# Last expert stage: each expert's weights in four transfers of 2 KB rows, and full and small places in turn

## The chip, the cores and the metric

One core of a Trainium2 chip runs the whole program. The metric is the device time of one execution in microseconds (us); lower is better. TensorE (PE) multiplies matrices, VectorE (DVE) and ScalarE (ACT) work on tiles, GpSimd (POOL) also issues the indexed transfers, and SyncE (SP) issues the plain ones. All transfers run on the core's 16 DMA engines.

## The reference

Two decoder layers over 32 sequences of 128 tokens with 256 features each, all in f32. Only the last part matters here: a mixture of experts in which each token goes to two of eight experts.

```python
xf = x.reshape(T, D)
gate_scores = jax.nn.sigmoid(gate_logits + balance_bias)
topk_scores, topk_idx = jax.lax.top_k(gate_scores, ACTIVE_EXPERTS)
...
h = jax.nn.silu(jnp.einsum('td,ehd->teh', xf, w1))
expert_out = jnp.einsum('teh,edh->ted', h, w2)
out = jnp.einsum('te,ted->td', comb, expert_out)
...
x = x + _L1_ffn_ref(_layernorm(x, axis=-1), ...)
```

Each expert has w1 of 512 x 256 and w2 of 256 x 512, together 1024 KB.

## The kernel before

The kernel runs its stages one after the other: a Mamba block, two attention blocks, a first expert stage (names with d_), a recurrence, an attention block (e_), and the last expert stage (f_). The last stage reuses the memory of earlier tiles, so nearly everything in it is called e_dead in the profile; its function is `list_experts`.

The rows of tokens were scattered before into `rows_in_place`, one region for each expert. The stage works through 40 **places** (`SLOTS`, numbered u = 0 to 39). A full place takes two tiles of 128 rows of one expert, a small place takes one. `list_plan` writes the list `PLACE_PLAN` of pairs (tiles, number of the first half unit): 21 full places from a first table that is filled early (`EARLY`), then, from the second table, 10 full places (u = 21 to 30) and 9 small ones (u = 31 to 39). Which expert and which rows a place has is only known at run time; some places are empty, and then all of their row numbers are out of bounds and nothing is added to the output. Empty places load their weights and compute all the same.

For each place u:

- SP loads its rows (272 KB for a full place, 136 KB for a small one, L2677) and its expert's weights (1024 KB in one transfer, 8 KB in each of 128 partitions, L2680) into a ring of `RING` = 3 buffers. The weights wait until PE has finished the down product of place u - 3, since they overwrite its buffer.
- PE makes the four up products (L2718, f = 0 to 3). After f = 0 of place u it makes the down product of place u - 1 (L2705, `output_tensor`), and after f = 1 it transposes the rows of place u + 1 (L2695, `turn_rows`). Each up product starts with a wait for the weights at f = 0.
- ACT applies SiLU (L2741) and copies the transposed rows (L2731).
- DVE reads each token's number (`f_token`, L2756) and multiplies each tile of the down product by the token's share (L2764, one for each tile). It writes into a ring of `OUT` = 4 buffers and waits there for the additions of place u - 4.
- POOL adds the tile to the output in memory by an indexed transfer with addition (L2778, two for a full place, one for a small one). It waits first until all additions of the places before have landed, since two places can hold the same token. The end of the program waits for the last of them.

```python
            for u in range(SLOTS):
                pl.wait_ge(mixed, upto[u + 1])
                ...
                after(pl, added, 16 * upto[u])
                for k in range(tiles[u]):
                    nc.gpsimd.indirect_dma_start(tokens_of, ...
```

Of the kernel before, what the change touches and what calls it, by code (L numbers as in the profile page):

```python
# [27 lines left out]
def after(eng, sem, count):  # L28

    if not isinstance(count, int) or count > 0:  # L30
        eng.wait_ge(sem, count)
# [97 lines left out]
def early_units(groups):  # L129

    rows = 2 * (groups - 1) * GT
    return -(-(rows - 8 * (UR - 1)) // UR)


def list_plan(groups):

    early = early_units(groups)
    halves = (2 * groups * GT - 8) // 128 + 8 - 2 * early
    single = 8 + halves % 2
    full = (halves - single) // 2  # L140
    plan = [(2, 2 * n) for n in range(early)] + [(2, 2 * n) for n in range(full)]
    return early, full, plan + [(1, 2 * full + n) for n in range(single)]


def slot_order(groups):
# [31 lines left out]
def decoder_kernel(nc, ins, out):  # L177
# [18 lines left out]
    E, REGION = 8, NG * GT  # L196
    RUNS = 2 * E + 1
    EARLY, FULL, PLACE_PLAN = list_plan(NG)
    SLOTS = len(PLACE_PLAN)
    PLACES = sum(split_units(NG)) - split_units(NG)[1] // 2  # L200
# [19 lines left out]
    w_in = m_w_sb[:, 0:1024].rearrange("p (k o) -> p k o", k=KD)  # L220
# [488 lines left out]
    def early_router(tag, mem, table, FB, SB, number, full, empty, x_in, plan):  # L709
# [236 lines left out]
        def late_table_vector(dve, at):  # L946
# [45 lines left out]
                  early=[16, 30, 48]),  # L992
# [8 lines left out]
    def attention(tag, turn, sets, relu=False, rms=None, out_w=None, table=None, result=None, ahead=None, begun=None, then=None, shared=None, base=0):  # L1001
# [721 lines left out]
        if table:  # L1723
            out_late = LAST["out_at"]
            last_sides = [lambda pe, p: [back_tensor(pe, NG - 1, p, [0], LAST["back"]), router["total_tensor"](pe, 0, LAST["total"])],
                          lambda dve, p: [back_vector(dve, NG - 1, p, [0], out_late), router["early_table_vector"](dve, LAST["early_table"])],
                          lambda act, p: [], lambda pool, p: []]
            end_sides = [lambda pe: [back_tensor(pe, NG - 1, 1, [1], LAST["back"]), router["total_tensor"](pe, 1, LAST["late_total"])],
                         lambda dve: [back_vector(dve, NG - 1, 1, [1], out_late), router["late_table_vector"](dve, LAST["late_table"])],
                         lambda act: [], lambda pool: []]  # L1730
            turn_of_list = turn + 4
            places = list_experts("f", mem, 0, table, result, dead, router, lambda sp: store_x(sp, NG - 1),
                                  ended=dict(mixed=(mixed, PAIRS * NG), drawn=(drawn, PAIRS * NG), shifted=(shifted, UNITS * NG),
                                             taken=(taken, UNITS * NG), valued=(valued, PAIRS * (NG - 1))))
            listed_places = [places[x] for x in ("tensor", "vector", "scalar", "pool")]
# [890 lines left out]
    def list_experts(tag, mem, turn, table, result, dead, router, store_rest, ended):  # L2626

        FC, UT = 4, UR // 128
        UPS, WN = KD * 512, KD * 512 + 4 * D
        RING, OUT = 3, 4  # L2630
        left = list(sem_set[turn])
        s = lambda name: ctx.enter_context(nc.semaphore(f"{tag}_{name}", num=left.pop(0)))
        t = lambda name, shape, dtype=F32: mem.take(f"{tag}_{name}", shape, dtype)
        w = dead[0][:, 0:RING * WN].rearrange("p (r n) -> p r n", r=RING)
# [10 lines left out]
        w_in, row_in = ([s(f"{n}{r}") for r in range(RING)] for n in ("w_in", "row_in"))  # L2645
# [17 lines left out]
        def sync(sp):  # L2663
            for u in range(SLOTS):
                r = u % RING
                if u == 0:
                    sp.wait_ge(ended["valued"][0], ended["valued"][1])
                    sp.wait_ge(in_list[0], ALL)
                    sp.wait_ge(in_list[1], ALL - 16 * router["scatters"])
                    sp.wait_ge(ready_places, 1)  # L2670
                if u == EARLY:
                    sp.wait_ge(in_list[1], ALL)
                    sp.wait_ge(ready_places, 2)
                after(sp, turned, u - RING + 1)
                after(sp, sent_to, u - RING + 1)
                at = sp.value_load(table["start_i"][:].unsqueeze(2)[0:1, u], min_val=0, max_val=E * REGION // 128)
                sp.dma_start(rows[:, r, 0:tiles[u]], rows_at[:, bass.ds(at, tiles[u])]).then_inc(row_in[r], 16)  # L2677
                e = sp.value_load(table["expert_i"][:].unsqueeze(2)[0:1, u], min_val=0, max_val=E - 1)
                after(sp, down, late(u - RING + 1))
                sp.dma_start(w[:, r], ins[f"{tag}_w"][e]).then_inc(w_in[r], 16)  # L2680
                if u == RING:
                    store_rest(sp)
            sp.wait_ge(stored, 16 * NG)

        def turn_rows(pe, u):
            pe.wait_ge(row_in[u % RING], 16 * (u // RING + 1))
            if u == 0:
                pe.wait_ge(ended["shifted"][0], ended["shifted"][1])
            if u == 1:
                pe.wait_ge(ended["mixed"][0], ended["mixed"][1])  # L2690
                pe.wait_ge(ended["drawn"][0], ended["drawn"][1])
            after(pe, turned_in, u)
            for c in range(KD):
                for k in range(tiles[u]):
                    step = nc.tensor.transpose(TB(u)[:, c, k * L:k * L + L], rows[:, u % RING, k, c * 128:c * 128 + 128], ident[:])  # L2695
            step.then_inc(turned, 1)

        def output_tensor(pe, u):
            pe.wait_ge(hidden, FC * u + FC)
            if u == 0:  # L2700
                pe.wait_ge(ended["taken"][0], ended["taken"][1])
            for r in range(tiles[u]):
                after(pe, mixed, had(u, r))
                for f in range(FC):
                    step = nc.tensor.matmul(DB(r), hid[:, u % 2, f, r * 128:r * 128 + 128], w_down[:, u % RING, f], start=f == 0, stop=f == FC - 1)  # L2705
                step.then_inc(down, 1)

        def tensor(pe):
            turn_rows(pe, 0)
            yield 0  # L2710
            for u in range(SLOTS):
                for f in range(FC):
                    if f == 0:
                        pe.wait_ge(w_in[u % RING], 16 * (u // RING + 1))
                        pe.wait_ge(turned_in, u + 1)
                    after(pe, hidden, FC * (u - 1) + f + 1)
                    for c in range(KD):
                        step = nc.tensor.matmul(UB(f)[:, 0:wide(u)], w_up[:, u % RING, c, f * 128:f * 128 + 128], xT[:, u % 2, c, 0:wide(u)], start=c == 0, stop=c == KD - 1)  # L2718
                    step.then_inc(up, 1)
                    if f == 0 and u:  # L2720
                        output_tensor(pe, u - 1)
                    if f == 1 and u + 1 < SLOTS:
                        turn_rows(pe, u + 1)
                    yield 10 * u + 2 * f + 2
            output_tensor(pe, SLOTS - 1)
# [41 lines left out]
        def pool(pl):  # L2767
# [13 lines left out]
            pl.wait_ge(added, 16 * upto[SLOTS])  # L2781

        return dict(sync=sync, tensor=tensor, scalar=scalar, vector=vector, pool=pool)


# [7 lines left out]
    u = lambda name, shape: u_mem.take(f"u_{name}", shape)  # L2793
# [16 lines left out]
    f = lambda name, shape, dtype=F32: f_mem.take(f"f_{name}", shape, dtype)  # L2810
# [191 lines left out]
```

## Time and profile before

| | |
|---|---|
| median of 3 runs | 3130.05 us (3126.87 to 3141.59) |
| the profiled execution, its time | 3133.9 us |
| its span | 3131.8 us |
| granted clock, mean | 0.952 of full |
| PE busy | 2695.4 us (86%) |
| last stage, first weights asked for to end | about 2834 to 3131.8 us |

The profile shows one execution. "Busy" is the time in which an engine executes; an engine's idle time before an instruction is put down to what released it. Times inside the trace count from the start of the span. DMA shares are of 16 engines: 50% means that each engine moved packets half of the time.

### The profile page before, as it was taken

To read this page: it belongs to the slowest core of one execution; us is meant where nothing else is said; L and a number is where in the kernel's file an instruction comes from. 1 tells how busy PE (TensorE), PEld (TensorE's weight loads), DVE (VectorE), ACT (ScalarE), POOL (GpSimd) and SP (SyncE) were. 2 spreads that over 40 slices of the span, in tenths; PEclk is the share of its full clock that TensorE was granted. 3 is DMA by queue.
4 is the path that set the end of the run, shared out by engine and by line. 5 is a ranking of instruction groups with operands and counts; after the bars stand their busy time and mean duration, and the time that the engine had idled before them with its cause. 6 is when DMAs were issued, how large, how long until landed. Compare 5 with 4: busy or idle time off the path is not lost.

```text
span 3131.8 us, 49455 instructions
## 1 busy us (share of the span) xinstructions
PE 2695.4 (86%) x16576; PEld 1837.2 (59%) x16576; DVE 1900.0 (61%) x3513; ACT 1523.1 (49%) x2641; POOL 1499.7 (48%) x1619
## 2 busy tenths in 40 slices
PE   5888888876988888879999999899888888878997
PEld 2333333323666566645788887697455555557886
DVE  3788888784888788863222222501688988883211
ACT  4566665553777666630122221443666666643322
POOL 3577666673555577625322222200345555553443
PEclk8999999988999999989999999899999999978998
DMA  9700000001005000002377775200000100006875
GB/s 324 245 0 1 0 1 1 1 0 37 15 20 190 1 1 0 1 22 95 117 212 209 209 212 146 71 1 1 1 18 30 37 33 31 22 20 188 228 216 167
DMA packets 137955, 244.73 MB, mean 78 GB/s; under 512 B 15936, under 2 KB 111424, under 8 KB 127040
## 3 DMA queue, kind: packets, MB, share of 16 engines
q1 hardware_dynamic: 111168, 207.61, 20.1%
q0 software_dynamic: 26592, 34.63, 5.6%
q8 instruction: 109, 1.79, 0.2%
q14 instruction: 86, 0.70, 0.1%
HBM read 151.28 MB, written 92.73 MB: 78 GB/s over the span
## 4 chain that ended last, share of the span: by engine, by line
PE 35%; DVE 6%; issue 6%; POOL 5%; ACT 2%; DMA 1%; another core or an unknown queue 0%; POOLq 0%; DVEq 0%; ACTq 0%
PE PS L2442 11%; PE PS L2398 6%; PE PS L2066 4%; PE PS L2705 3%; PE PS L2718 3%; POOL e_hs L1544 2%; DMA out<-e_dead,f_token 1%; DVE e_mx L1447 1%; POOL e_qs L1547 1%; PE PS L1399 1%; POOL rows_in_place L878 1%; PE PS L2057 1%; PE PS L1337 1%; DVE e_pr L1451 1%; DVE e_den L1458 1%
## 5 line engine op out<-in xcount | busy, mean ns | idle before, releaser
L578 POOL TENSOR_TENSOR u_in<-dtx,b_rep 128x512 f32<-128x512 f32 x256 | 325.4, 1294 | 201.3 <-ACT b_rep L559 200.1
L594 DVE TENSOR_TENSOR_SCAN state<-PS,u_in 128x512 f32<-128x512 f32 x256 | 312.3, 1220 | 59.3 <-POOL u_in L578 34.9
L551 PE MATMUL PS<-scaled,ident 128*128 128x512 f32 x512 | 295.6, 661 | 28.7 <-DVE scaled L588 28.7
L2459 ACT ACTIVATE d_act_b<-PS 128x256 f32<-128x256 f32 (+2 forms) x192 | 76.5, 400 | 446.4 <-PE PS L2442 426.4
L1544 POOL TENSOR_TENSOR e_hs<-e_pr 128x512 f32<-128x512 f32 x128 | 163.0, 1273 | 236.5 <-ACT e_pr L1511 232.9
L1544 POOL TENSOR_TENSOR u_hs<-u_pr 128x512 f32<-128x512 f32 x128 | 166.3, 1299 | 215.1 <-ACT u_pr L1511 214.6
L2442 PE MATMUL PS<-d_unit_T,d_w 128*128 128x256 f32 (+1 forms) x1280 | 260.6, 356 | 1.1 <-ACT d_unit_T L2452 1.1
L2362 POOL DMA_INDIRECT out_by_token<-d_y_rows,d_token x71 | 110.8, 1561 | 300.2 <-DVE d_y_rows L2489 201.6
L2468 DVE TENSOR_TENSOR d_hid<-d_act_b,PS 128x256 f32<-128x256 f32 (+2 forms) x192 | 84.4, 441 | 279.9 <-ACT d_act_b L2459 245.6
L567 ACT ACTIVATE PS<-dt,decay_rate 128x508 f32<-128x508 f32 x256 | 173.4, 686 | 138.0 <-DVE state L594 136.2
L2442 PEld LDWEIGHTS PS<-d_unit_T,d_w 128*128 128x128 f32 x1280 | 221.0, 190 | 26.3 <-DVE d_hid L2468 1.3
L588 DVE TENSOR_TENSOR scaled<-state,PS 128x512 f32<-128x512 f32 x256 | 169.4, 664 | 55.9 <-PE PS L532 44.3
L1447 DVE TENSOR_REDUCE u_mx<-PS 128x8 f32<-128x1024 f32 x128 | 155.9, 1218 | 67.9 <-PE PS L1390 67.8
L2398 PE MATMUL PS<-d_w,d_hid 128*128 128x256 f32 x824 | 186.8, 380 | 3.6 <-DVE d_hid L2468 2.6
L2778 POOL DMA_INDIRECT out<-e_dead,f_token x71 | 110.8, 1561 | 158.1 <-DVE f_token L2756 68.2
L1507 ACT ACTIVATE e_pT<-PS 128x1024 f32<-128x1024 f32 x128 | 130.8, 1022 | 103.2 <-PE PS L1399 103.2
L1447 DVE TENSOR_REDUCE e_mx<-PS 128x8 f32<-128x1024 f32 x128 | 155.8, 1217 | 40.6 <-PE PS L1390 40.5
L2398 PEld LDWEIGHTS PS<-d_w,d_hid 128*128 128x128 f32 x824 | 155.6, 190 | 30.2 <-issue 7.5
L1399 PE MATMUL PS<-ident,e_pr 128*128 128x128 f32 x1024 | 148.2, 292 | 25.8 <-ACT e_pr L1511 25.3
L1507 ACT ACTIVATE u_pT<-PS 128x1024 f32<-128x1024 f32 x128 | 131.2, 1025 | 74.2 <-PE PS L1399 73.9
L551 PEld LDWEIGHTS PS<-scaled,ident 128*128 128x128 f32 x512 | 97.2, 204 | 117.9 <-DVE scaled L588 87.1
L1451 DVE TENSOR_TENSOR u_pr<-PS,u_mx 128x1024 f32<-128x1024 f32 x128 | 156.7, 1224 | 9.3 <-POOL u_hs L1544 2.2
(453 smaller groups left out, 6145.2 us busy)
## 6 DMA issues: line engine op xcount, KB each, us to landing
d_w<-in_d_w SPq DMA_DIRECT2D x42, 1024.0 KB, 5.8
e_dead<-in_f_w SPq DMA_DIRECT2D x40, 1024.0 KB
rows_in_place<-blank SPq DMA_DIRECT2D x136, 272.0 KB, 4.1
d_w<-in_d_w SPq DMA_DIRECT2D x42, 512.0 KB
rows_by_expert<-zeros SPq DMA_DIRECT2D x36, 272.0 KB, 3.1
d_unit_rows<-rows_by_expert SPq DMA_DIRECT2D x31, 272.0 KB
e_dead<-rows_in_place SPq DMA_DIRECT2D x31, 272.0 KB
X<-in_x SPq DMA_DIRECT2D x8, 512.0 KB, 11.2
```

What stands on the lines that cost most here:

```text
L551: nc.tensor.matmul(YB[:, c], ident[:], scaled[:, (KD * n + c) % RC], start=False, stop=n == NS - 1).then_inc(m_y, 1)
L567: nc.scalar.activation(seqs(DECAY[:, k % RD])[:, :, 1:L], seqs(dt[:, p, c])[:, :, 1:L], ACT.Exp, scale=decay_rate[:, c * NS + n:c * NS + n ...
L578: nc.gpsimd.tensor_tensor(u_in[:, k % RU], dtx[:, p, c], b_rep[:, n % RB], ALU.mult).then_inc(m_u, 1)
L588: nc.vector.tensor_tensor(scaled[:, k % RC], state[:, k % 2], CB, ALU.mult).then_inc(m_hc, 1)
L594: nc.vector.tensor_tensor_scan(state[:, k % 2], DECAY[:, k % RD], u_in[:, k % RU], 0.0, ALU.mult, ALU.add).then_inc(m_h, 1)
L1399: step = nc.tensor.transpose(TR[:, m], pr[:, i % 2, m], ident[:])
L1447: nc.vector.tensor_reduce(mx[:, i % 2], scores_of(i), AX.X, ALU.max).then_inc(maxed, 1)
L1451: nc.vector.tensor_tensor(pr[:, i % 2], scores_of(i), mx[:, i % 2].unsqueeze(2).broadcast_to([128, MAPS, L]), ALU.subtract).then_inc(shift ...
L1507: nc.scalar.activation(pT[:, i % 2].rearrange("p h q -> p (h q)"), flat(PS[:, 4:6]), ACT.Copy).then_inc(taken, 1)
L1544: nc.gpsimd.tensor_tensor(hs[:, i % 2], pr[:, i % 2, :, 0:L // 2], pr[:, i % 2, :, L // 2:L], ALU.add).then_inc(halved, 1)
L2398: step = nc.tensor.matmul(out_h[:, n], hid[:, p, f, row:row + 128], w_down[:, r, f], start=f == 0, stop=f == FC - 1)
L2442: step = nc.tensor.matmul(b, wt[:, r, c, f * 128:f * 128 + 128], x, start=c == 0, stop=c == KD - 1)
```

## The change

Two edits. The weights of a place come in four transfers of 512 columns (256 KB, 2 KB in each partition) in place of one, and PE waits for all four. And in the second table the small places stand between the full ones: after u = 22 they take turns, small, full, small, and so on to u = 39, which is small. The number of places, the half units that they name and the sums stay as they are.

```diff
     single = 8 + halves % 2
     full = (halves - single) // 2
-    plan = [(2, 2 * n) for n in range(early)] + [(2, 2 * n) for n in range(full)]
-    return early, full, plan + [(1, 2 * full + n) for n in range(single)]
+    plan = [(2, 2 * n) for n in range(early)]
+    pairs, ones = [(2, 2 * n) for n in range(full)], [(1, 2 * full + n) for n in range(single)]
+    alone = max(full - single, 0)
+    plan += pairs[:alone]
+    for n in range(single):
+        plan += pairs[alone + n:alone + n + 1] + ones[n:n + 1]
+    return early, full, plan
...
-        RING, OUT = 3, 4
+        RING, OUT, PARTS = 3, 4, 4
...
-                sp.dma_start(w[:, r], ins[f"{tag}_w"][e]).then_inc(w_in[r], 16)
+                for c in range(PARTS):
+                    part = slice(c * WN // PARTS, (c + 1) * WN // PARTS)
+                    sp.dma_start(w[:, r, part], ins[f"{tag}_w"][e][:, part]).then_inc(w_in[r], 16)
...
-                        pe.wait_ge(w_in[u % RING], 16 * (u // RING + 1))
+                        pe.wait_ge(w_in[u % RING], 16 * PARTS * (u // RING + 1))
```

PE before, at the passage from the last full place (u = 30) to small ones near the end of the program (L2718 up product, L2705 down product, L2695 transposes of the next rows; 128x256 is a full place's up product and 128x128 a small one's):

```order
L2718 MATMUL PS<-e_dead 128x256 x2
L2695 MATMUL PS<-ident,e_dead 128x128 x2
L2718 MATMUL PS<-e_dead 128x256 x4
L2718 MATMUL PS<-e_dead 128x128 x2
L2705 MATMUL PS<-e_dead 128x256 x8
L2718 MATMUL PS<-e_dead 128x128 x2
L2695 MATMUL PS<-ident,e_dead 128x128 x2
L2718 MATMUL PS<-e_dead 128x128 x6
L2705 MATMUL PS<-e_dead 128x256 x4
```

PE after, near the end of the program (line numbers are 7 higher):

```order
L2725 MATMUL PS<-e_dead 128x256 x2
L2702 MATMUL PS<-ident,e_dead 128x128 x2
L2725 MATMUL PS<-e_dead 128x256 x4
L2725 MATMUL PS<-e_dead 128x128 x2
L2712 MATMUL PS<-e_dead 128x256 x8
L2725 MATMUL PS<-e_dead 128x128 x2
L2702 MATMUL PS<-ident,e_dead 128x128 x4
L2725 MATMUL PS<-e_dead 128x128 x4
L2725 MATMUL PS<-e_dead 128x256 x2
L2712 MATMUL PS<-e_dead 128x256 x4
```

What before stood there once now stands nine times: a small place's first up product ahead of a full place's down product, and in the small place the transposes of a full place's rows (x4).

SP before, one small place (f_start_i and f_expert_i are the tables of starts and experts; the waits name semaphores by their numbers' first owners):

```order
L2676 TENSOR_LOAD f_start_i [waits m_nb,m_padded]
L2676 ISA x2
L2677 ISA
L2677 DMA e_dead<-rows_in_place 128x272
L2678 TENSOR_LOAD f_expert_i
L2678 ISA x2
L2680 ISA [waits m_vec2]
L2680 DMA e_dead<-in_f_w 128x2048
```

SP after, the same place's weights:

```order
L2687 ISA [waits m_vec2]
L2687 DMA e_dead<-in_f_w 128x512
L2687 ISA
L2687 DMA e_dead<-in_f_w 128x512
L2687 ISA
L2687 DMA e_dead<-in_f_w 128x512
L2687 ISA
L2687 DMA e_dead<-in_f_w 128x512
```

One wait still stands ahead of the weights; three transfers more stand behind it, ahead of the rows of the next place.

## Rows read from the trace of the kernel before

**Rows 1.** Busy time by stretch (columns PE, PEld, DVE, ACT, POOL, clock, DMA share, GB/s).

```profile
3000.00:3050.00 50.00, 50.00 (x247) 44.05 (x246) 9.04 (x35) 15.37 (x42) 20.66 (x14) 1.00 0.76 218
```

**Rows 2.** PE in order of time (start, duration): a full place's parts, down products, waits.

```profile
3001.89 0.60 PE L2695 MATMUL PS<-ident,e_dead 128*128 128x128 f32 x4
3002.33 2.76 PE L2718 MATMUL PS<-e_dead 128*128 128x256 f32 x12
3004.92 3.62 PE L2705 MATMUL PS<-e_dead 128*128 128x256 f32 x16
...
3063.69 3.62 PE L2705 MATMUL PS<-e_dead 128*128 128x256 f32 x16
...
3070.59 3.72 PE L2705 MATMUL PS<-e_dead 128*128 128x256 f32 x16
...
3076.23 1.99 PE L2705 MATMUL PS<-e_dead 128*128 128x256 f32 x8
...
3084.06 1.99 PE L2705 MATMUL PS<-e_dead 128*128 128x256 f32 x8
...
3105.46 0.71 PE L2718 MATMUL PS<-e_dead 128*128 128x128 f32 x4 [0.90 <-DMA e_dead<-in_f_w]
3109.60 1.99 PE L2705 MATMUL PS<-e_dead 128*128 128x256 f32 x8 [0.37 <-ACT e_dead L2741]
```

**Rows 3.** DVE: the second tile of u = 30.

```profile
3074.35 0.48 DVE L2764 TENSOR_SCALAR e_dead<-PS,f_share_rows 128x256 f32<-128x256 f32 x1 [1.14 <-PE PS L2705]
```

**Rows 4.** POOL's indexed additions in order of time, with the idle time before.

```profile
3017.74 1.55 POOL L2778 DMA_INDIRECT out<-e_dead,f_token  x1 [4.49 <-DMA out<-e_dead,f_token]
...
3041.08 1.56 POOL L2778 DMA_INDIRECT out<-e_dead,f_token  x1 [0.30 <-issue]
3047.72 1.55 POOL L2778 DMA_INDIRECT out<-e_dead,f_token  x1 [5.08 <-DMA out<-e_dead,f_token]
...
3075.67 1.55 POOL L2778 DMA_INDIRECT out<-e_dead,f_token  x1 [3.10 <-DVE f_token L2756]
...
3123.12 1.55 POOL L2778 DMA_INDIRECT out<-e_dead,f_token  x1 [2.02 <-DMA out<-e_dead,f_token]
```

**Rows 5.** The chain that ended last: additions (start, time from issue to landing).

```profile
3077.53 5.92 DMA out<-e_dead,f_token
3084.31 3.82 DMA out<-e_dead,f_token
3088.99 7.26 DMA out<-e_dead,f_token
...
3107.06 3.82 DMA out<-e_dead,f_token
...
3119.54 2.72 DMA out<-e_dead,f_token
```

**Rows 6.** DMA queues (packets, MB, share) in 3075.67:3084.2, then in 3119.54:3123.1.

```profile
q1 hardware_dynamic: 598, 2.56, 80.8%
q0 software_dynamic: 288, 0.00, 1.9%
...
q0 software_dynamic: 144, 0.00, 2.0%
```

**Rows 7.** Other loads: queue q1 in 792:798 (one 512 KB load), then SP.

```profile
q1 hardware_dynamic: 272, 0.52, 25.1%
...
993.89 12.37 SPq L2863 DMA_DIRECT2D out_by_token<-zeros  x16
...
747.08 0.43 SPq L1134 DMA_DIRECT2D c_wk<-in_c_wk  x1
747.55 0.53 SPq L1134 DMA_DIRECT2D c_wv<-in_c_wv  x1
```

**Rows 8.** The first weights: SP's issue, and PE's weight load that waited for them.

```profile
2833.86 0.37 SPq L2680 DMA_DIRECT2D e_dead<-in_f_w  x1
2839.90 1.93 PEld L2718 LDWEIGHTS PS<-e_dead 128*128 128x128 f32 x8 [0.62 <-DMA e_dead<-in_f_w]
```

## The prediction

> **What bounds the kernel now.** I read the page first, then the busy time by stretch, PE in order of time, POOL in order of time and the chain that ended last. The change touches only the last stage, from about 2834 us to the end at 3131.8. In its middle PE is busy in all of the 50 us between 3000 and 3050, at full clock, while the DMA engines stand at a share of 0.76 [rows 1]. The down products of u = 21 and u = 29 start at 3004.92 and 3063.69 [rows 2]: eight full places in 58.77 us, 7.35 us each, with no gap. From the starts at 3001.89, 3002.33 and 3004.92 [rows 2], transposes take 0.44, three up products 2.59 (0.86 each), and the down product the other 3.45; a small place's parts are half of it, some 0.45, 0.22 and 1.73, together 3.74. No transfer decides there.
>
> The end is different. PE starts its last down product at 3109.60 [rows 2] and is done at 3111.6, but the last addition is only issued at 3123.12 [rows 4]. The chain runs over additions, one after another [rows 5]. Call L the time from the issue of a place's last addition to its landing. POOL starts the next place 0.86 us after a landing: 3084.31 + 3.82 = 3088.13, next start 3088.99 [rows 5]. So a small place takes POOL 0.86 + L, and a full one 1.86 us more for its first addition (3077.53 less 3075.67, [rows 4, 5]). With L = 3.8 to 7.3, nine small places in a row need 4.7 to 8.1 us each; PE makes one in 3.915 us (3076.23 to 3084.06 for two, [rows 2]). POOL falls behind through the whole run, and the program ends with POOL: 3123.12 + 2.72 for an empty place as in [rows 5] = 3125.8, and 6 us of closing after it.
>
> **What lengthens L.** Two empty places compare directly. The addition at 3077.53 belongs to u = 30, which moved 0.00 MB [rows 6], and took 5.92 us. The one at 3119.54 is empty too, with nothing beside it, and took 2.72 [rows 5, 6]. The difference is 3.20 us. Each addition is 144 packets, 9 on each of 16 engines [rows 6]. Beside the first, queue q1 used 80.8% of 8.53 us for 2.56 MB, 0.16 MB an engine: 6.9 us, or 0.35 us for 8 KB. Nine packets that each wait behind one 8 KB weight packet wait 3.15 us. That is the difference. With 2 KB rows the same count gives 9 x 0.09 = 0.8 us.
>
> **The change, part by part.** (1) *2 KB rows.* Engine time per byte: the 512 KB load of 2 KB rows took 25.1% of 6 us on q1, 1.5 us, so 350 GB/s [rows 7]; the 8 KB rows above ran at 0.16 MB in 6.9 us on 16 engines, 370 GB/s, partly other packets. I take no loss; the bound above is 6% of some 3 us a place, which PE's full places hide. Separate transfers do not queue badly either: 16 stores of 256 KB were issued in 12.37 us [rows 7], 0.77 us each.
>
> (2) *SP.* Issues without a register read stand 0.47 us apart [rows 7]. Three more for each place cost 1.4 us, and the register step ahead of each some 0.03. The last quarter of the weights is asked for 1.4 us later; SP then takes the next rows. In turns, the weights of a full place have 11.3 us less the 1.95 of a small down product and 0.86 of an up product, 8.4 us; those of a small place 11.3 - 3.6 - 0.45 = 7.2 us. The longest wait shown is that of u = 39, whose weights were needed at 3104.5 and came at 3105.46 [rows 2]. The first weights of the stage took 6.04 us with the ring otherwise nearly empty (2833.86 to 2839.90) and PE's weight load waited 0.62 us for them [rows 8]. At worst 6.04 + 1.4 = 7.4 exceeds 7.2 by 0.2, nine times: 0 to 2 us; I take 0, since the queue moves the first quarters while SP issues the last. At the stage's start the cover is thin: 0 to 1.4 us, I take 0.5. If it slipped at each of 40 places it would be 56 us, but a full place has 10 us for it (7.35 x 2 less 3.6 and 0.86) and hides it.
>
> (3) *The turns, on PE.* In the small run PE lost 2.3 us to weights: from 3084.06 to 3109.60 are 25.54 us, against 6 x 3.915 less the 0.22 of the last place's missing transposes, 23.27 [rows 2]. These waits go. Against it, a small up product (0.45 us) is now the only cover ahead of a full down product: from 3063.69 to 3070.59 are 6.90 us [rows 2] where shorter work (7.35 - 0.43 - 0.22) gives 6.70, 0.2 lost on ACT. That happens nine times, not once, but the small places' own ACT gap of 0.17 goes with each (3.915 against 3.74): +0.03 for each pair, so 11.29 us a pair. PE's last tile is handed to POOL at about 3110.3: that of u = 22 starts at 3004.92 + 7.35 - 0.22 = 3012.05 (before: 3012.27), that of u = 38 at 3012.05 + 8 x 11.29 = 3102.4, then 3.45, three small up products with ACT's gap 1.86, and 2.61 to DVE's end.
>
> (4) *The turns, on POOL.* A full place hands over its tiles 4.24 us after its down product starts (3070.59 to 3074.35 + 0.48 = 3074.83, [rows 2, 3]), and POOL starts 0.84 later [rows 4]. A pair needs (0.86 + 1.86 + L) + (0.86 + L) = 3.58 + 2L of POOL against 11.29 of PE. They are equal at L = 3.86. Which L? The lone addition at 3107.06 took 3.82 with data [rows 5]; that is the floor. In the full places before, L reached 5.8 (3041.08 to 3047.72 less 0.86, [rows 4]); it was about 4.6 on the average of the twelve from 2985 on, as near as their waits show, 0.8 over the floor where 3.2 were possible. A quarter of that, for 0.8 possible, is 0.2, so **L = 4.05**, and 3.0 for places with little or nothing in them.
>
> From u = 22, whose additions start at 3017.74 [rows 4], to the end POOL has nine full places (9 x 1.86 = 16.7), 17 steps of 0.86 (14.6), 14 places with data and 4 short ones (u = 35 and the last three): 3017.7 + 31.3 + 14 x 4.05 + 4 x 3.0 = **3117.7**. Sum: 3125.8 becomes 3117.7 + 0.5 from the start = 3118.2, that is -7.6 us; with a small lag in both, -7. The profiled execution of 3133.9 would be 3127; it lies 3.9 us above the median, so against 3130.05 the forecast is **3123 us**, -0.22%.
>
> **A rule against it.** The 256 KB transfers of [rows 7] stand 0.77 us apart. The Trainium skill ("DMA: Bandwidth & Descriptors", section Bandwidth) says to batch transfers to at least 1 MiB to reach three quarters of the peak; its section on the anatomy of one DMA fits 2.0 us plus the bytes at 436 GB/s to each, for GpSimd's transfers. An estimate from that page for four quarters in series is 4 x 2.6 = 10.4 us against 4.4 for one transfer. By that rule the change would lose if the fixed parts added up; the trace's 0.77 us shows them overlapped.
>
> **Rivals.**
> - *L stays near 4.6* (3.7 when empty), because additions wait for something other than packet length. For it: 7.26 at 3088.99 [rows 5] is more than floor plus 3.15. Against: the two empty places. End: 3017.7 + 31.3 + 64.4 + 14.8 = 3128.2, later than before by 2.4: 3133. Nothing gained, the turns having moved POOL's lag forward.
> - *Weights late in the turns.* Price 0.5 to 1 us for each pair through PE and 1.4 at the start: PE's end 3115 to 3119, the end 3121 to 3126; time 3126 to 3132.
> - *Slower: transfers in series.* If a quarter's fixed time adds up (say the 2.7 us of an empty addition [rows 5] for each of three more, 8.1 us), weights take 14 us against the 10 us of a full place and PE waits 4 us at some 38 places: +150 us, 3280. It decides from 4 us more a transfer. [Rows 7] speak against.
> - *POOL never lags* (L = 3.82, 2.72): the end is PE's, 3102.4 + 4.24 + 0.84 + 1.86 + 2.72 + 0.86 + 2.72 = 3115.6. That is -10: 3120.
> - *Only the turns act, and well.* Without the short rows, L with data at 4.6 and empty at 3.5: 3127.4, that is +1.6; so this can't give a gain.
>
> **How the numbers follow.** Chances: forecast 0.50 (3120 to 3126, its own range), no lag 0.10 (3118 to 3121), L unchanged 0.18 (3129 to 3135), weights late 0.14 (3126 to 3132), transfers in series 0.04, something that the rows don't show 0.04. The medians themselves spread (3126.87 to 3141.59 in three runs), which widens both ends. The range 3118 to 3133 leaves out the series case, half of the unknown, and the top of the unchanged one. 0.5% is 15.7 us, about what a measurement here can tell from no change. More than 12 us can't come from this part: PE's last work stands at 3110. So faster by over 0.5% has 0.03, slower 0.06, within it 0.91.
>
> **What would show it.** In the new profile: the additions' landing times around 4 us instead of up to 7.3; POOL's last start within 6 us of PE's last matmul, not 11.5; no wait of L2725 for in_f_w in the second table; pairs of 11.3 us on PE; q1's packets in the stage four times as many, with the same engine time. The first weights' wait grows from 0.62 to about 1. Wrong would be: L of 4.6 and more beside 2 KB packets, a DMA share of the full places above 0.9, or waits for weights in them.

## The result

Before: median 3131.12 us (3125.62 to 3141.59, 15 runs). After: **3146.11 us** (3138.51 to 3149.08, 15 runs), ratio **1.0039** with the 95% interval 1.003 to 1.0047. By the ratio the kernel is some 12 us slower (the medians lie 15 us apart) where 7 us less were forecast, and the time lies above the range. The change does what it says: the turns and the four transfers are there. The kernels of the experiments ran on several chips, whose medians of the kernel before lie between 3131 and 3140 us; so they are compared by their ratios to it.

The profiled execution took 3149.08 us. Its page and its busy time by stretch (PE, PEld, DVE, ACT, POOL, clock, DMA share, GB/s):

```profile
span 3147.3 us, 49815 instructions
PE 2703.6 (86%) x16576; PEld 1842.9 (59%) x16576; DVE 1901.9 (60%) x3513; ACT 1522.3 (48%) x2641; POOL 1499.6 (48%) x1619
```

```profile
3000.00:3050.00 50.00, 49.73 (x263) 43.59 (x262) 9.76 (x38) 14.57 (x48) 17.90 (x13) 1.00 0.87 235
3050.00:3100.00 50.00, 42.88 (x233) 37.24 (x231) 8.13 (x33) 13.86 (x47) 14.73 (x10) 1.00 0.73 197
3100.00:3106.00 6.00, 5.85 (x22) 4.96 (x23) 0.00 (x0) 0.28 (x1) 1.69 (x2) 0.72 0.96 235
```

PE has the same 16576 matmuls. From 3000 to 3050 it is as busy as in [rows 1]; in the next 50 us it idles for 7. PE in order of time, which answers to [rows 2]:

```profile
3005.68 3.62 PE L2712 MATMUL PS<-e_dead 128*128 128x256 f32 x16
3012.58 3.72 PE L2712 MATMUL PS<-e_dead 128*128 128x256 f32 x16
...
3024.09 3.72 PE L2712 MATMUL PS<-e_dead 128*128 128x256 f32 x16
...
3083.16 0.71 PE L2725 MATMUL PS<-e_dead 128*128 128x128 f32 x4 [1.52 <-DMA e_dead<-in_f_w]
...
3091.92 1.13 PE L2725 MATMUL PS<-e_dead 128*128 128x256 f32 x4 [2.82 <-DMA e_dead<-in_f_w]
...
3100.15 0.79 PE L2725 MATMUL PS<-e_dead 128*128 128x128 f32 x4 [2.56 <-DMA e_dead<-in_f_w]
3100.73 5.27 PE L2712 MATMUL PS<-e_dead 128*128 128x256 f32 x16
...
3116.49 0.71 PE L2725 MATMUL PS<-e_dead 128*128 128x128 f32 x4 [3.00 <-DMA e_dead<-in_f_w]
...
3124.05 1.99 PE L2712 MATMUL PS<-e_dead 128*128 128x256 f32 x8 [0.37 <-ACT e_dead L2748]
```

The first pair (3012.58 to 3024.09) takes 11.51 us, close to the forecast 11.29. Then weights come late, four times by 1.5 to 3.0 us. After the first two of these waits the granted clock stays at 1.00 (3083 to 3095). After the last two it falls (0.72 from 3100 to 3106, 0.50 of it from 3101 to 3103, which is the 1.2 GHz level), and a full down product takes 5.27 us in place of 3.62. PE starts its last down product at 3124.05, 14.45 us later than in [rows 2]. POOL is later still: its last addition goes out at 3138.60, against 3123.12 in [rows 4], and is again what the end waits for. The additions in the chain that ended last (start, time to landing), from u = 22 on, which answer to [rows 5]:

```profile
3020.40 6.91 DMA out<-e_dead,f_token
...
3028.17 6.30 DMA out<-e_dead,f_token
...
3037.18 4.18 DMA out<-e_dead,f_token
...
3051.17 6.77 DMA out<-e_dead,f_token
...
3083.73 7.99 DMA out<-e_dead,f_token
...
3092.58 5.14 DMA out<-e_dead,f_token
...
3100.43 7.35 DMA out<-e_dead,f_token
...
3135.02 2.73 DMA out<-e_dead,f_token
```

The chain has one such row for each of the 17 places u = 22 to 38. The first eleven sum to 68.5 us, so **L = 6.2 us** on the average where the forecast had 4.05; the other six are 3.6 to 3.8 with data and 2.7 without. All 17 sum to 87.7 us; with 2.7 for u = 39, 90.4, against the forecast 68.7. That is 21.7 us of the 23.6 by which the last landing (3138.60 + 2.7 = 3141.3) misses the forecast 3117.7. The rest is the start (0.8) and 1 us between landings and next additions.

Two sides of the same lag, from the waits in the stage, 2835 to 3147 (engine, line, what was waited for: us in total, times, longest):

```profile
POOL out L2785 <- DMA out<-e_dead,f_token: 93.8, 25, 6.2
DVE f_token L2763 <- DMA out<-e_dead,f_token: 45.7, 9, 9.7
...
PE PS L2725 <- DMA e_dead<-in_f_w: 10.4, 6, 3.0
```

How DVE's wait reaches PE is seen around 3083 to 3092. First DVE, then SP, in order of time:

```profile
3081.04 0.15 DVE L2763 CAST f_token<-e_dead 128x1 int32<-128x1 f32 x1 [4.86 <-DMA out<-e_dead,f_token]
...
3091.75 0.17 DVE L2763 CAST f_token<-e_dead 128x2 int32<-128x2 f32 x1 [9.67 <-DMA out<-e_dead,f_token]
```

```profile
3020.98 1.88 SPq L2687 DMA_DIRECT2D e_dead<-in_f_w  x4
...
3032.49 1.88 SPq L2687 DMA_DIRECT2D e_dead<-in_f_w  x4
...
3051.16 1.88 SPq L2687 DMA_DIRECT2D e_dead<-in_f_w  x4
...
3083.14 1.88 SPq L2687 DMA_DIRECT2D e_dead<-in_f_w  x4
3092.72 0.33 SPq L2682 DMA_DIRECT2D e_dead<-rows_in_place  x1
3093.81 1.88 SPq L2687 DMA_DIRECT2D e_dead<-in_f_w  x4
```

The addition of 3083.73 lands at 3091.72. At 3091.75 DVE may read the next token numbers, since the ring of `OUT` = 4 was full; that releases the row buffer, SP asks for the next rows at 3092.72 and, behind them in its order, for weights at 3093.81. PE needs those and gets them at 3100.15. So once POOL is four places behind, the landings of the additions set when weights are asked for.

### The profile page after: what moved, and what is told of

It is laid out like the page before. It is cut to its first block, busy times and chain, and to the rows that moved or that the text cites. A ratio compares the mean times of both kernels' runs of the same rounds, so it can differ in the third digit from the quotient of the medians.

```text
span 3147.3 us, 49815 instructions
## 1 busy us (share of the span) xinstructions
PE 2703.6 (86%) x16576; PEld 1842.9 (59%) x16576; DVE 1901.9 (60%) x3513; ACT 1522.3 (48%) x2641; POOL 1499.6 (48%) x1619
## 4 chain that ended last, share of the span: by engine, by line
PE 29%; POOL 7%; issue 7%; DVE 7%; DMA 6%; ACT 2%; POOLq 0%; SPq 0%; DVEq 0%; ACTq 0%
PE PS L2447 11%; PE PS L2403 6%; DMA out<-e_dead,f_token 5%; PE PS L2071 4%; POOL e_hs L1549 3%; POOL e_qs L1552 1%; DVE e_mx L1452 1%; POOL out L2785 1%; PE PS L1404 1%; POOL rows_in_place L883 1%; PE PS L2062 1%; DVE e_pr L1456 1%; PE PS L1342 1%; DVE e_den L1463 1%; PE PS L2712 1%
## 5 line engine op out<-in xcount | busy, mean ns | idle before, releaser
L1404 PEld LDWEIGHTS PS<-ident,e_pr 128*128 128x128 f32 x1024 | 125.5, 151 | 63.0 <-ACT e_pr L1516 55.1
```

Source lines behind the costliest of these rows:

```text
L1404: step = nc.tensor.transpose(TR[:, m], pr[:, i % 2, m], ident[:])
```

## The experiments

**1. Each edit alone.** `e1_turns` has the new order and one transfer (`PARTS = 1`); `e2_parts` has the order of before and four transfers.

```diff
-        RING, OUT, PARTS = 3, 4, 4
+        RING, OUT, PARTS = 3, 4, 1
```

> Only the turns; the weights come in one transfer of 8 KB rows as before. Theory A (an addition waits for the whole weight burst that is already queued, whatever its rows; the turns put a full place's second addition right behind the next weights, so POOL needs more than PE's 11.3 us a pair, falls four places behind, and then DVE's read of the token numbers and with it SP's next rows and weights wait): 8 to 16 us slower than before, with the same PE waits for weights of 1 to 3 us in the last pairs. Theory B (the quarters make the weights late, the turns are harmless): within 3 us of before.

> Only the four transfers of 2 KB rows; the order of places as before. Theory A: 0 to 4 us slower than before (the start 0.7, and later weights in the run of small places). Theory B: 10 to 16 us slower. Were the prediction's step on packets right (short packets let additions through), it would be 3 to 6 us faster.

Measured: e1_turns 1.0063 (1.005 to 1.0076); e2_parts 1.0006 (0.9995 to 1.0017). The loss belongs to the turns: some 20 us, more than the 8 to 16 that theory A gave. The four transfers of 2 KB rows take a part of it back when they are there; alone they are worth nothing that can be told. In the chain of e1_turns the last additions of u = 22 and u = 26 (start, time to landing):

```profile
3022.59 9.50 DMA out<-e_dead,f_token
...
3056.56 8.63 DMA out<-e_dead,f_token
```

Over u = 22 to 32 the eleven rows of that chain give L = 6.8 (74.7 / 11). In the chain of e2_parts the eight full places u = 22 to 29 have L = 4.5 (36.1 / 8). The forecast's step from 4.6 to 4.05 was worked out for just such places, and it is not there. And the empty place u = 30, on whose two additions the forecast was built, in the chain of e2_parts and in its DMA queues from 3074.41 to 3081.7:

```profile
3069.49 4.07 DMA out<-e_dead,f_token
...
3076.27 5.36 DMA out<-e_dead,f_token
...
3082.48 5.87 DMA out<-e_dead,f_token
```

```profile
q1 hardware_dynamic: 1201, 2.07, 93.2%
q0 software_dynamic: 288, 0.00, 2.2%
```

Beside 2 KB rows it took 5.36 us; the forecast's count of packets gives 2.72 + 0.8 = 3.5, and 8 KB rows had 5.92 [rows 5]. So an addition does not wait for one weight row with each of its packets.

**2. The changed kernel again, and with a deeper ring.** `after_again` is the changed kernel, on the chip of experiment 4. `e3_out8` is the changed kernel with eight output buffers, `e7_turns_out8` the same with one transfer, `e10_before_out8` the kernel before with eight.

```diff
-        RING, OUT, PARTS = 3, 4, 4
+        RING, OUT, PARTS = 3, 8, 4
...
-        y = dead[1][:, 3072:5120].rearrange("p (o k d) -> p o k d", o=OUT, k=UT)
+        y = dead[1][:, 3072:7168].rearrange("p (o k d) -> p o k d", o=OUT, k=UT)
```

> The changed kernel itself, beside the others on one chip. All theories: 8 to 16 us slower than before (it measured a ratio of 1.0039), the turns alone having been 1.0063.

> The changed kernel with eight output buffers in place of four (OUT = 8), so DVE and SP are held only when POOL is eight places behind. Theory A: PE's waits for weights in the last pairs (some 10 us in all) go, and the end is POOL's chain alone: 4 to 10 us faster than the changed kernel, still not faster than before. Theory B: no change against the changed kernel, the waits for weights stay.

> The turns alone (8 KB rows) with eight output buffers in place of four. Theory A: the coupling through the output buffers turns POOL's lag into PE waits, so without it PE's waits for weights fall from some 9 us to below 3, and the loss against before falls from 20 us to 8 to 14 us, what is left being POOL's chain of long landings. Rival (weights late for a reason of their own): PE's waits stay at 9 us and the time at that of e1_turns.

> The order and the transfers of before, with eight output buffers in place of four. In before, PE waits some 2 us for weights in the run of small places, behind DVE's held read of token numbers. Theory A: these waits go, but the end is POOL's chain, so the time is within 3 us of before. Rival (before, too, loses through the coupling): 4 us or more faster.

Measured: after_again 1.0052 (1.0035 to 1.0069); e3_out8 1.004 (1.0026 to 1.0053); e7_turns_out8 1.0027 (1.0009 to 1.0045); e10_before_out8 0.9993 (0.9976 to 1.001). With eight buffers DVE's read of the token numbers waits no more, and in the turns PE loses nothing more to late weights. In e7_turns_out8 the first weights were asked for 4.7 us earlier than in [rows 8] (2829.20), and PE starts its last down product 4.8 us earlier than in [rows 2]: PE needs just as long. Yet POOL, shown behind it, is 25 us later than PE:

```profile
3104.82 1.99 PE L2712 MATMUL PS<-e_dead 128*128 128x256 f32 x8 [0.37 <-ACT e_dead L2748]
```

```profile
3129.77 1.55 POOL L2785 DMA_INDIRECT out<-e_dead,f_token  x1 [2.02 <-DMA out<-e_dead,f_token]
```

So in the turns the waits of PE are a consequence: they go, and POOL's chain of additions still makes the turns slower than before. The order of before is different. There e10_before_out8 has the time that was expected, but PE's waits for weights didn't go: 4.9 us in three waits, against 1.9 in the profile before. With DVE's waits gone they are still there, so theory A had their cause wrong. The longest, 2.8 us, ends at 3078.51, and from 3074 to 3078 the DMA engines are busy throughout (a share of 1.01). The ring of four buffers does add to the loss in the one-transfer kernel (1.0063 against 1.0027, intervals apart). In the changed kernel itself the medians don't show it (1.0039 and 1.0052 against 1.004, where 4 to 10 us were expected), though L over u = 22 to 32 falls from 6.2 to 5.5 in the profile (60.1 / 11); its share there stays open.

**3. Row length and number of transfers apart.** `e4_rows2k` has the order of before and one transfer of 2 KB rows, the weights being laid out in memory as four blocks; `e9_turns_1of2k` the same in the turns; `e8_turns_4of8k` has the turns and four transfers of 32 partitions with 8 KB rows.

```diff
-                sp.dma_start(w[:, r], ins[f"{tag}_w"][e]).then_inc(w_in[r], 16)
+                sp.dma_start(w[:, r].rearrange("p (c n) -> p c n", c=4), ins[f"{tag}_w"][e].rearrange("c p n -> p c n")).then_inc(w_in[r], 16)
```

```diff
-                    part = slice(c * WN // PARTS, (c + 1) * WN // PARTS)
-                    sp.dma_start(w[:, r, part], ins[f"{tag}_w"][e][:, part]).then_inc(w_in[r], 16)
+                    part = slice(32 * c, 32 * c + 32)
+                    sp.dma_start(w[part, r], ins[f"{tag}_w"][e][part]).then_inc(w_in[r], 16)
```

> One transfer for a place's weights as before, but cut into 2 KB rows by the layout in memory (four blocks of 512 columns for each expert); the order of places as before. Theory A: the size of a row changes nothing, within 2 us of before, additions beside weights still take up to 6 to 7 us to land. The prediction's step: landings beside weights at 4.5 us at most, 3 to 6 us faster than before.

> The turns with four transfers for a place's weights, each of 32 partitions with 8 KB rows (the changed kernel has four of 128 partitions with 2 KB rows). So far the turns cost 0.63% with one transfer of 8 KB rows and 0.39 to 0.52% with four of 2 KB rows. If the number of transfers is what lets additions in between, this kernel is like the changed one (12 to 17 us slower than before); if the length of a row is, it is like the turns alone (18 to 24 us slower). I expect the number.

> The turns with one transfer for a place's weights, in 2 KB rows (blocks in memory as in e4_rows2k). If the number of transfers counts: 18 to 24 us slower than before, landings up to 9 us. If the length of a row counts, as the prediction had it: 12 us or less.

Measured: e4_rows2k 0.9994 (0.9981 to 1.0006); e8_turns_4of8k 1.0082 (1.0057 to 1.0106); e9_turns_1of2k 1.0047 (1.0032 to 1.0063). The number of transfers, which I had expected to count, does nothing here that can be told. In the turns it is the rows that count: 1.0063 and 1.0082 with 8 KB, 1.0039 to 1.0052 with 2 KB, each with one and with four transfers. On one chip e8 and e9 have medians of 3160.12 and 3146.94 us. The loss of e9, 15 us, lies between the two that were expected. L over u = 22 to 32, in one profile of each, says the same: 6.8 and 6.9 (75.4 / 11 in e8) with 8 KB, 6.2 and 6.4 (70.1 / 11 in e9) with 2 KB. A quarter of the row length takes off some 0.5 us, where the forecast's count wanted three quarters of all that lies above the floor. In the order of before it is worth nothing; there the empty place u = 30 took even 6.42 us beside 2 KB rows of one transfer.

**4. Without the weights.** Both load only 32 of the 2048 columns of the weights; the loads of rows, 136 or 272 KB a place, are left. `e6_before_light` has the order of before, `e5_turns_light` the turns, each with one transfer.

```diff
-                sp.dma_start(w[:, r], ins[f"{tag}_w"][e]).then_inc(w_in[r], 16)
+                sp.dma_start(w[:, r, 0:32], ins[f"{tag}_w"][e][:, 0:32]).then_inc(w_in[r], 16)
```

> The turns with one transfer for a place's weights that brings only 32 of the 2048 columns (the other weights are left out, so the output is not the reference's); PE's and POOL's work is the same. Theory A (the loss comes from additions that wait for weight bursts): landings of 2.7 to 3.8 us everywhere, a pair takes POOL 11.2 us against PE's 11.3, no waits for weights; 8 to 12 us faster than before and 2 to 6 us faster than e6_before_light. Rival (the turns cost by themselves, through ACT, DVE or the order of waits): at least 8 us slower than e6_before_light.

> The order of before with the same 32 columns of weights alone (the rest is left out). Theory A: the run of small places costs POOL 4.7 us each in place of 4.7 to 8.1; 4 to 8 us faster than before. Rival: if bursts do not lengthen landings, within 3 us of before.

Measured: e5_turns_light 0.9967 (0.9953 to 0.9981), e6_before_light 0.9966 (0.9949 to 0.9983). Without weights the turns lose nothing, so they hurt by where they put the additions beside the weights. They win nothing either: the gain of 2 to 6 us over e6_before_light that was expected even here is not there to be measured. On PE it has a reason. The pair of places takes 11.51 us in e5_turns_light too (down products at 3017.04 and 3028.55), 0.22 more than the forecast's 11.29. From the first up product to the start of the last down product PE needs 269.6 us there, in e6_before_light 267.5 and before 269.7: the turns cost PE about what its waits for weights had cost it, and in e5_turns_light the chain that ended last runs over PE. The lowest L shows in the chain of e6_before_light, from the same empty place u = 30 on, behind u = 28 and u = 29:

```profile
3064.52 5.15 DMA out<-e_dead,f_token
3072.39 3.83 DMA out<-e_dead,f_token
3078.93 2.80 DMA out<-e_dead,f_token
3082.59 3.69 DMA out<-e_dead,f_token
3087.13 3.61 DMA out<-e_dead,f_token
3091.59 3.86 DMA out<-e_dead,f_token
3096.31 3.73 DMA out<-e_dead,f_token
```

2.80 us, against 5.92, 5.36 and 6.42 with weights in one or the other form; and u = 31 to 34 at 3.6 to 3.9, where before had up to 7.26 [rows 5]. There the difference is due to the weights. But not all is: u = 28 and u = 29 have the same L with the weights as without. Before, in the chain that ended last:

```profile
3063.12 5.17 DMA out<-e_dead,f_token
3071.01 3.81 DMA out<-e_dead,f_token
```

In these two places of the row of full ones, the weights that were asked for 3.0 and 3.5 us ahead of the addition add nothing, and shorter rows have nothing to win. In u = 25 they do add: 5.8 before [rows 4], at most 4.6 here (3042.49 to the next start at 3047.97, less 0.86). What makes the 5.2 of u = 28 stays open. Leaving out the weights is worth 0.34% in all.

The empty place u = 30 also shows that the moment counts. In e10_before_out8, with full weights in 8 KB rows, its second addition comes late, 7.0 us after one place's weights were asked for (3074.30) and 1.5 us ahead of the next (3082.80):

```profile
3081.35 2.72 DMA out<-e_dead,f_token
```

That is as short as with nothing beside it. Before, 3.1 us after weights and 0.9 ahead of the next, it took 5.92.

**5. The weights spread out in time.** By now I held that an addition suffers from a burst: 1 MB asked for at once. Then four quarters spread over the place should let it through. `e11_turns_spread` (from the changed kernel) and `e12_before_spread` (from e2_parts) hold back each of the last three quarters until PE has made a certain up product of place u - 2 or, for the last quarter, of place u - 1.

```diff
                 for c in range(PARTS):
+                    if u >= RING and c:
+                        sp.wait_ge(up, FC * (u - 2) + (0, 2, 4, FC + 1)[c])
                     part = slice(c * WN // PARTS, (c + 1) * WN // PARTS)
```

> The changed kernel, with the four quarters of a place's weights spread in time: SP waits with the second for up product f = 1 of place u - 2, with the third for f = 3, with the last for f = 0 of place u - 1. Theory A (an addition waits behind the weights queued as one burst): a burst is at most two quarters, 1.5 us in place of 3, so landings stay below some 5 us, POOL falls behind by less than four places, and the loss against before falls from 12 to 17 us to between -4 and +6 us. Rival (only the share of the DMA engines counts, not how it is bunched): as the changed kernel.

> The order of before with the four quarters spread in the same way. Theory A: landings of full places below 4.5 us; in the run of small places the weights may come late, since a last quarter has 3.9 us less the down product. Between 4 us faster and 6 us slower than before. Rival: as e2_parts, within 3 us of before.

Measured: e11_turns_spread 1.0125 (1.0099 to 1.0151), e12_before_spread 1.0127 (1.0098 to 1.0156), both some 38 us slower than before, and alike. The theory of the burst fell, and so did both rivals, that nothing would change. SP and then the chain of additions in e12_before_spread, in the first table and, the last row, at u = 24:

```profile
2940.23 4.55 SPq L2684 DMA_DIRECT2D e_dead<-in_f_w  x4
...
2947.58 4.22 SPq L2684 DMA_DIRECT2D e_dead<-in_f_w  x4
```

```profile
2972.32 6.26 DMA out<-e_dead,f_token
...
2981.30 5.58 DMA out<-e_dead,f_token
...
2989.59 5.39 DMA out<-e_dead,f_token
...
3061.09 7.29 DMA out<-e_dead,f_token
```

A place's weights are now asked for over 4.2 to 4.6 of the 7.35 us of a full place, and every place's second addition meets them: L = 5.4 to 6.6 in the full places from 2972 to 3033, and up to 7.35 later. The places from 2972.32 to 2981.30 and on to 2989.59 take POOL 9.0 and 8.3 us against PE's 7.35, so POOL falls behind from the first table on. The order of the places no longer matters. POOL is late first and PE only then. In e12_before_spread PE runs from 2850 to 3038 without a wait for weights, while DVE's reads of token numbers wait for additions from 2978.61 on. Behind that PE waits 33.1 us for weights, in e11_turns_spread 26.5. Whether these waits would go with eight buffers was not tried; in the run of small places the late last quarter may cost time by itself. What the first table shows is that the same bytes, asked for over a longer time, made L longer, not shorter.

## Why the prediction was wrong

**The step that failed** is "What lengthens L", and with it the **L = 4.05** of step (4). The difference of two empty places (3.20 us) agreed with nine waits of 0.35 us, and I took the agreement for the mechanism. It was a coincidence: with 2 KB rows the same place took 5.36 and 6.42 us, not 3.5. Shown: L is 2.7 to 2.8 (empty) or mostly 3.6 to 3.9 (data, once 5.15) without weights; with them it is 3.7 to 9.7, 6.2 on the average of the changed kernel's first eleven places from u = 22 on; shorter rows take off some 0.5 us in the turns and nothing in the order of before.

**The phase.** The forecast carried one L from the row of full places into the turns. What goes with a long L is when the place's last addition goes out against the weights. In the row of full places of e2_parts the weights of 3065.96 were asked for 3.53 us before the addition of 3069.49, which took 4.07. In the turns: weights at 3020.98 and an addition at 3020.40, 6.91; at 3051.16 and 3051.17, 6.77; at 3083.14 and 3083.73, 7.99; but 3032.49 and 3037.18, 4.7 us behind them, 4.18. It is no strict rule: at 3058.79, 3.1 us behind the weights, L is 5.85. SP's quarters go out when a down product ends. After a full place's product its second addition follows some 3.5 us later; in the turns the small place's product that ends next asks for weights just then. PE's order fixes this phase, and where POOL lags and `OUT` = 4 binds, the landings themselves do. That both coincide is seen in the rows. That the weights beside the additions are the price was shown by taking them out (experiment 4), and the empty place at two moments fits it; how L follows from the distance was not measured by itself.

**The step that was missing** is the price of a lag. A pair asks 3.58 + 2L of POOL; with L = 6.2 that is 16 us against PE's 11.5. The five pairs from the addition at 3020.40 to the one at 3100.43 took 16.0 us each. The forecast knew that the two break even at L = 3.86, a hair from the floor, and so had no margin. What follows when POOL is four places behind (DVE, SP, weights, PE, clock) it left out.

**The rivals.** "L stays near 4.6" was nearest: no gain from short rows, POOL's lag moved forward. Its L was right for the order of before (4.5 in e2_parts) and wrong for the turns, and so was its price, 2.4 us instead of 15.5. "Weights late in the turns" came true (10.4 us of waits in place of 2.3), but by POOL's lag, not by slower transfers, and POOL's own end lies later still. "Transfers in series" did not come: e2_parts is level. "POOL never lags" fell with the weights there.

**The steps that held.** (1) 2 KB rows cost no time: e4_rows2k is level. Engine time rose with four transfers, though: from 2920 to 3000 queue q1 of the changed kernel used 58.8% for 14.52 MB, before 53.8% for 14.61 MB, 10% more for each byte, while one transfer of 2 KB rows in e4_rows2k used 53.0% for 14.38. The full places hid it. (2) SP's three more issues: 1.88 us for four, as forecast 1.4 more, and hidden but for the start. (The forecast's cover of 8.4 us for a full place's weights is 8.5 by its own numbers; nothing rests on it.) There PE's weight load waited 0.80 us for the first weights and 0.55 for the second, and u = 21's down product starts 0.76 us later than in [rows 2]; 0.5 was forecast. (3) The pair on PE was 11.51 us while weights came in time, 0.22 above the forecast, 1.8 us over the eight pairs. The first weights, in answer to [rows 8]:

```profile
2839.97 2.20 PEld L2725 LDWEIGHTS PS<-e_dead 128*128 128x128 f32 x8 [0.80 <-DMA e_dead<-in_f_w]
...
2844.89 0.73 PEld L2725 LDWEIGHTS PS<-e_dead 128*128 128x128 f32 x4 [0.55 <-DMA e_dead<-in_f_w]
```

## What to carry to other kernels

When two transfer streams share the engines, what one costs the other depends on when they meet; an average read in one order of the work is not valid in another, so read from the trace which issue goes out when. If an order leaves an engine within a few tenths of a microsecond of its limit, price the case in which it falls behind, and follow it through the rings to the other engines. And a count that explains one difference exactly is a guess until a second size is seen: the kernel with only the four transfers would have told.

## What the runs showed of the hardware

With next to no weights moving (e6_before_light) an indexed addition of one tile landed 2.7 to 2.8 us (all rows left out) or 3.6 to 3.9 us after its issue, once 5.15. Beside loads of 1 MB it took up to 9.66 us (e7_turns_out8) and 9.50 (e1_turns), though the tile has only 128 KB. This holds for an empty one too: 5.92, 5.36 and 6.42 us, so the wait does not need data of its own. In two places an addition and weights landed together: in the changed kernel the addition of 3083.73 at 3091.72, and the weights for which PE waited, asked for at 3083.14, at 3091.92; in e10_before_out8 the addition of 3069.61 at 3078.64, and the weights for which PE waited at 3078.51. The Trainium skill ("DMA: Bandwidth & Descriptors", section Queues, rings and completion order) says that an engine changes between queues only at packet boundaries, a packet holding several descriptors, and that a transfer's semaphore update lands only after all earlier writes of that engine, over all its queues. The common landing fits the second. How much the first has to do with the small worth of short rows, no run here tells. None isolates either, so the mechanism stays open.

Cutting the same bytes into quarters that are asked for later made additions slower, not faster: L of 5.4 to 7.35 in the full places of e12_before_spread, and a program 38 us longer.
